# Two changes to a two-layer decoder kernel on one Trainium2 core: two layer norms as a pipeline of quarters, and a quarter of the recurrence's B products moved from GpSimd to ScalarE and TensorE

## The reference

```
def _selective_scan(u, dt, A, Bm, Cm, Dp):      # 4 blocks, 256 channels, 16 states
    dA  = exp(dt[..., None] * A)
    dBu = (dt * u)[..., None] * Bm[:, :, None, :]
    step: h = dA_t * h + dBu_t;  y = einsum('ben,bn->be', h, C_t)
    return y + u * Dp
...
x = x + L1_attn(_layernorm(x))        # four blocks, then a final _layer_norm(x, fn_w, fn_b)
x = x + L1_xattn(ctx_1024, _layernorm(x), mask)
```

## Time and profile before

| | |
|---|---|
| time, median of 3 runs | 1748.06 us (1745.92 to 1748.16) |
| the profiled execution's own time | 1755.21 us |
| its span (first to last instruction) | 1753.4 us |
| recurrence, first scan to last C product | 503.4 to 1348.5 us |
| final norm's stage | from 1356.8 us |
| second cross attention's stage | from 1370.8 us, its first masked score at 1388.9 us |
| busy | DVE 1428.6, PE 1318.3, POOL 1140.6, ACT 1100.6 us |

### The profile page before, as it was taken

How to read it: one execution, slowest core, us unless ns; L and a number is a source line. 1 busy time by engine, 2 the same in 40 slices (tenths; PEclk the granted TensorE clock), 3 DMA queues, 4 the chain that set the end, 5 groups by cost and what they waited for, 6 DMA issues and landing times. The chain is left out here.

```text
span 1753.4 us, 23313 instructions
## 1 busy us (share of the span) xinstructions
PE 1318.3 (75%) x6907; PEld 649.4 (37%) x6907; DVE 1428.6 (81%) x2430; ACT 1100.6 (63%) x2435; POOL 1140.6 (65%) x742
## 2 busy tenths in 40 slices
PE   6787898986666657676576685667655699999989
PEld 4554565553322212222122221222211366666543
DVE  4654888987359999999999999999997588877834
ACT  4444887876566666666666765666743687777730
POOL 2101565651069999999999999999996154444500
PEclk9999999998888888888888888888867899999979
DMA  3000000000054543454543534533430511121000
GB/s 102 1 1 2 1 2 1 1 3 24 6 212 176 193 164 122 169 179 171 194 154 128 195 138 190 194 146 127 176 144 23 175 49 50 50 95 49 1 1 24
DMA packets 70215, 168.03 MB, mean 96 GB/s; under 512 B 20420, under 2 KB 40152, under 8 KB 56664
## 3 DMA queue, kind: packets, MB, share of 16 engines
q1 hardware_dynamic: 68680, 166.17, 25.8%
q10 hardware_dynamic: 1168, 0.53, 0.1%
q0 software_dynamic: 256, 0.01, 0.0%
HBM read 131.04 MB, written 35.65 MB: 95 GB/s over the span
## 5 line engine op out<-in xcount | busy, mean ns | idle before, releaser
L1646 POOL TENSOR_TENSOR ma_hs<-ma_dtuR,ma_Bt 128x1024 f32<-128x1024 f32 x256 | 597.3, 2364 | 7.1 <-DMA ma_dtuR<-ma_dtu_d 6.9
L1829 ACT ACTIVATE ps<-ma_dtR,ma_A 128x512 f32<-128x512 f32 x512 | 332.7, 682 | 297.2 <-DVE ma_hs L1974 254.7
L852 POOL TENSOR_TENSOR x_pr<-x_pr,x_rec 128x512 f32<-128x512 f32 x256 | 267.9, 1047 | 273.5 <-DVE x_rec L1098 273.5
L1968 DVE TENSOR_TENSOR_SCAN ps<-ps,ma_hs 128x1024 f32<-128x1024 f32 x176 | 401.5, 2281 | 0.2
L1723 PE MATMUL ps<-ma_hs,ma_fold 128*32 128x512 f32 x1024 | 176.3, 822 | 206.8 <-POOL ma_hs L1654 178.1
L1064 ACT ACTIVATE x_pr<-x_sm,x_mx 128x256 f32<-128x256 f32 x512 | 255.3, 500 | 69.8 <-DVE x_mx L1089 66.2
L1974 DVE TENSOR_TENSOR ma_hs<-ps,ma_Ct 128x1024 f32<-128x1024 f32 x176 | 215.5, 1224 | 6.1
L1968 DVE TENSOR_TENSOR_SCAN ma_hs<-ps,ma_hs 128x1024 f32<-128x1024 f32 x80 | 182.5, 2281 | 18.4 <-ACT ps L1829 15.5
L1654 POOL TENSOR_TENSOR ma_hs<-ma_hs,ma_Ct 128x1024 f32<-128x1024 f32 x80 | 188.7, 2358 | 11.8 <-DVE ma_hs L1968 11.7
L1690 PE MATMUL ps<-ma_hn,ma_w_tap 128*128 128x512 f32 (+3 forms) x256 | 142.1, 708 | 50.0 <-ACT ma_hn L1853 50.0
L914 PE MATMUL ps<-ident,x_pr 128*128 128x128 f32 x1024 | 161.7, 284 | 5.5 <-DVE x_pT L995 4.4
(11 more groups left out here) (304 smaller groups left out, 2181.1 us busy)
## 6 DMA issues: line engine op xcount, KB each, us to landing
ma_dtuR<-ma_dtu_d SPq DMA_DIRECT2D x32, 1024.0 KB, 6.7
ma_dtR<-ma_dt_d SPq DMA_DIRECT2D x32, 1024.0 KB, 8.9
ma_Bt<-ma_bc_d SPq DMA_DIRECT2D x16, 1024.0 KB, 5.0
ma_Ct<-ma_bc_d SPq DMA_DIRECT2D x16, 1024.0 KB, 7.4
ma_dtu_d<-ma_dtu SPq DMA_DIRECT2D x32, 256.0 KB, 2.0
ma_dt_d<-ma_dt SPq DMA_DIRECT2D x32, 256.0 KB, 2.3
keys_d<-ma_kv SPq DMA_DIRECT2D x32, 256.0 KB, 4.4
values_d<-ma_kv SPq DMA_DIRECT2D x32, 256.0 KB, 3.2
```

Of the source, the lines that this page charges most:

```text
L852: pool.tensor_tensor(pr[:, r, :, :], pr[:, r, :, :], rec[:, r, :].unsqueeze(2).broadcast_to([P, 2, L]), ALU.mult).then_inc(pr_done, 1)
L1646: pool.tensor_tensor(hs[:, k % SLOTS, :, :], dtuR[:, unit(f, h), q, :].unsqueeze(1).broadcast_to([P, 2, CH]), rows(Bt, k), ALU.mult).then_ ...
L1829: e = act.activation(c.ps[:, 2 * (k % 2) + a, :], dtR[:, unit(f, h), q, :], ACT.Exp, scale=A[:, (f // QUARTERS) % 2, h, q, no:no + 1])
L1968: dve.tensor_tensor_scan(out, pair(k), slot(k), 0.0, ALU.mult, ALU.add).then_inc(scan_done, 1)
```

## The change

Two edits. **Norms:** the stage n5 is gone. The cross attention stage runs both norms itself (`TwoNorms`), quarter by quarter over three tiles of its own: the second norm's centre matmul of a quarter starts when VectorE has added that quarter's first norm. GpSimd adds the bias `fn_b` to `xT` beforehand (`shift`), and VectorE does gain and sum in one instruction (`add`). The first projection waits for quarter 0 alone, the first scores for quarter 1; quarters 2 and 3 are scaled on VectorE after the first and second head. The prefetch is issued by the cross attention's SP queue, and the clears (now those of the first cross attention too) move to the norm stage n4 ahead of the recurrence.

**B products:** of a step's 16 B products, the last four (`TURNED` = 12 to 15) are no longer GpSimd's. TensorE turns B and dt x u so that tokens lie on the partitions; ScalarE makes scaled copies of them (`scale_rows`, 32 of 128x128 for a step, spread over t = 0 to 10 by `SCALED`), reading every fourth element and writing every fourth; TensorE turns the products back (`turn_rows`, eight 128x128 transposes for an item) into `pair(k)`. For these items the decays go to `slot(k)`, and the scan takes its inputs from PSUM. The C products are split anew: VectorE's items in a step are 1, 2, 3, 4, 6, 7, 8, 11, 15 (nine), GpSimd's are 0, 5, 9, 10, 12, 13, 14 (seven). `dtR` and `dtuR` hold two halves instead of three.

```diff
+class TwoNorms:
+    def centre(self, pe, n, h):
+        if n:
+            pe.wait_ge(done, self.base + h + 1)
+        pe.matmul(c.ps[:, h, :], c.centre[:, :], (c.xT if n else c.xn)[:, h * CH:(h + 1) * CH], ...)
+    def average(self, pe, n, h):
+        pe.wait_ge(squared, self.base + 4 * n + h + 1)
+        pe.matmul(c.ps[:, 7 - h, :], c.average[:, :], self.sq[:, h, :], ...)
+    def shift(self, pool, h, biased):
+        pool.tensor_tensor(cols, cols, c.fn[:, 1:2].broadcast_to([P, CH]), ALU.add).then_inc(biased, 1)
+    def add(self, dve, h, biased):
+        dve.wait_ge(rstd_done, self.base + h + 1)
+        dve.tensor_tensor(self.shifted[:, h, :], c.ps[:, h, :], self.rstd[:, h, :], ALU.mult).then_inc(scaled, 1)
+        dve.wait_ge(scaled, h + 1)
+        dve.wait_ge(biased, h + 1)
+        dve.scalar_tensor_tensor(out=cols, in0=self.shifted[:, h, :], scalar=c.fn[:, 0:1], in1=cols, ...).then_inc(done, 1)
+    def scale(self, dve, h):
+        dve.wait_ge(rstd_done, self.base + 4 + h + 1)
+        dve.tensor_tensor(c.xn[:, ...], c.ps[:, h, :], self.rstd[:, h, :], ALU.mult).then_inc(done, 1)
 # cross attention, TensorE
+                    for h in range(4):
+                        norms.centre(pe, 0, h)
+                    for h in range(4):
+                        norms.average(pe, 0, h)
+                    norms.centre(pe, 1, 0)
+                    for h in range(3):
+                        norms.centre(pe, 1, h + 1)
+                        norms.average(pe, 1, h)
                     pe.wait_ge(c.wq1_in, 16)
+                    norms.wait(pe, 1)
                 for n in range(NP if small else 1):
                     project(0, n, True, False)
+                if not small:
+                    norms.average(pe, 1, 3)
 # cross attention, ScalarE
+                    square(0,0..3); inv_std(0,0); inv_std(0,1); inv_std(0,2); square(1,0); inv_std(0,3)
+                    square(1,1); inv_std(1,0); square(1,2); inv_std(1,1); square(1,3)
+                    (then the projection's evacuation, inv_std(1,2), inv_std(1,3))
 # recurrence
-    NORM_D = set(range(16)) - {0, 4, 6, 10, 14}
+    NORM_D = set(range(16)) - {0, 5, 9, 10, 12, 13, 14}
+    TURNED = {12, 13, 14, 15}
+    SCALED = (3, 5, 0, 1, 3, 3, 2, 4, 2, 5, 4, 0, 0, 0, 0, 0)
 # GpSimd
-                        if k + AHEAD < NK:
+                        if k + AHEAD < NK and not by_tensor(k + AHEAD):
                             times_b(k + AHEAD)
 # TensorE
+                def turn_rows(k):
+                    pe.wait_ge(rows_done, 32 * (f + 1))
+                    if on_vector(k - 2):
+                        pe.wait_ge(c_vector, n_vector(k - 2) + 1)
+                    else:
+                        pe.wait_ge(scan_done, k - 1)
+                    for a in range(2):
+                        for t in range(4):
+                            mm = pe.transpose(c.ps[:, 2 * (k % 2) + a, t * P:(t + 1) * P],
+                                              rowB[:, t, a, q, :, :].rearrange("p e n -> p (e n)"), c.ident[:, :])
+                    mm.then_inc(turned, 1)
                     if F < NF:
                         pe.wait_ge(dt_done, 2 * F + 2)
+                        turn_b(F)                        # 4 small transposes into PA
 ...
                         kv_job(4 * f + 2, Y[0])
+                    if 0 <= f < NF:
+                        turn_rows(f * ITEMS + 12)
                     if G < NF:
                         if f >= 1:
                             pe.wait_ge(resid, f)
                         average(G)
                     if 0 <= f < NF:
+                        turn_rows(f * ITEMS + 13)
                         sum_y(f, 2)
+                        turn_rows(f * ITEMS + 14)
                         pe.wait_ge(kv_done, 4 * f + 3)
                         kv_job(4 * f + 3, Y[0])
+                    if 0 <= f < NF:
+                        turn_rows(f * ITEMS + 15)
+                    if F < NF:
+                        turn_dtu(F)                      # 4 transposes into PB
 # ScalarE
+                    if by_tensor(k):
+                        act.wait_ge(y_done, (k - SLOTS) // 4 + 1)
+                    elif k >= 2:
 ...
+                def scale_rows(f, i):
+                    t, a, ni = i // 8, i // 4 % 2, i % 4
+                    act.activation(rowB[:, t, a, :, :, ni], dtuT[:, t, :].rearrange("p (e q) -> p q e", q=GQ), ACT.Copy,
+                                   scale=BT[:, f % 2, t, a, ni:ni + 1]).then_inc(rows_done, 1)
+                        if F < NF and t == 9:
+                            copy_b(F)                    # bank PA to BT
+                        if F < NF and t == 15:
+                            copy_dtu(F)                  # bank PB to dtuT
+                        for _ in range(SCALED[t]):
+                            scale_rows(f, made)
```

More of the change, by code:

```diff
@@ L892, in score_pair @@
                         pe.wait_ge(k_in[p], b * 8 + 16 - 8 * p)
+                        if first:
+                            norms.wait(pe, 2)
                     if small and (n >= 4 or not first):
@@ L908, in turn @@
                 def turn(b, n, first):
+                    if not small and first and n < 2:
+                        norms.wait(pe, n + 3)
                     pe.wait_ge(pr_done, b * NH + n + 1)
@@ L1000, in _ @@
             def _(act):
-                norm.on_scalar(act)
+                if small:
+                    norm.on_scalar(act)
+                else:
+                    act.preload_act_table_set("natural_log_exp_and_others")
+                    for h in range(4):
+                        norms.square(act, 0, h)
+                    norms.inv_std(act, 0, 0)
+                    norms.inv_std(act, 0, 1)
+                    norms.inv_std(act, 0, 2)
+                    norms.square(act, 1, 0)
+                    norms.inv_std(act, 0, 3)
+                    norms.square(act, 1, 1)
+                    norms.inv_std(act, 1, 0)
+                    norms.square(act, 1, 2)
+                    norms.inv_std(act, 1, 1)
+                    norms.square(act, 1, 3)
                 def evacuate(b, p, n, first, second):
@@ L1033, in _ @@
                     evacuate(0, 0, n, True, False)
+                if not small:
+                    norms.inv_std(act, 1, 2)
+                    norms.inv_std(act, 1, 3)
                 if small:
@@ L1076, in _ @@
             def _(dve):
-                norm.on_vector(dve)
+                if small:
+                    norm.on_vector(dve)
+                else:
+                    for h in range(4):
+                        norms.add(dve, h, biased)
+                    for h in range(2):
+                        norms.scale(dve, h)
                 def maximum(b, p, n, first):
@@ L1147, in body @@
                         maximum(b, p, n, first)
+                        if masked_rows and first and n < 2:
+                            norms.scale(dve, n + 2)
                         step(b, p, n, first)
@@ L1469, in on_vector, with by_tensor, n_times_b, n_turned @@
         return k % ITEMS in NORM_D
+    def by_tensor(k):
+        return k % ITEMS in TURNED
+    def n_times_b(k):
+        return k - n_turned(k)
+    def n_turned(k):
+        return sum(by_tensor(a) for a in range(k))
     def n_vector(k):
```

176 lines of the change are left out of this document (130 added, 46 removed).

## The result

The changed kernel takes **1736.72 us** (median of 5 runs, 1724.17 to 1738.99) against 1748.06 in the same comparison; the ratio is 0.9914 [0.9886, 0.9943]. The medians lie 11.3 us apart, the ratio stands for 15 us, and its interval (10 to 20 us) holds both. Forecast were 1713 us, a ratio of 0.980, 35 us less: the sign and the range (1693 to 1738) hold, the size doesn't. The profiled execution took 1737.79 us with a span of 1736.1, against 1755.21 and 1753.4 before.

What follows compares the result with a forecast made beforehand. VectorE and GpSimd were both taken as full in the recurrence, with VectorE alone setting the pace after the change. Terms -40 + 10 + 8 + 1 - 13.5 = -35 us gave 1713 us from 1748.1; range 1693 to 1738.

Steps and rivals of the forecast that it cites:

- Norms: Cross attention stage: VectorE starts the first masked score at T+17.2 instead of T+32.1; -13.5 us, from -15 to -9.
- VectorE's gain: Recurrence: VectorE gives up two C products a step, 2.5 us each step, -40 us over 16 steps.
- The B products that remain are in time: GpSimd in the recurrence: products 16 and 17 made 3 us or more before their scans, 18 about 1.3.
- Decay of item 4: ScalarE: late C product 14 delays sum, tap projection, silus and this decay; 0.5 us a step, +8 us, ends 0 and 1.5.
- the gate: VectorE, t = 1: due 5.7 us after scan 0; the awaited sum ends at 4.7, or 6.4 at the lower clock.
- Turn 14: TensorE, behind `sum_y(f,2)`: 0.6 us late for its scan each step, +10 us, ends 0 and 2.5 us a step.
- the first rival: TensorE may stay at 2.4 GHz, so all turns and projections are hidden: 1695 us, chance 0.22.
- the B products' half: Recurrence: -40 + 10 + 8 + 1, forecast at -21 us.
- Scaled copies: ScalarE: 32 copies a step at 0.30 us each, 9.6 us; they cost nothing while VectorE's items cover them.
- ScalarE did not become the bound: Rival on ScalarE: at about 0.55 us a copy it becomes the bound, only norms gain: 1735 us; chance 0.15, shared.
- All hidden: Rival on TensorE: all turns and projections hidden, 1748 - 40 - 13.5 = 1695 us, chance 0.22.
- the sum, 1713: Whole kernel: all terms together give -35 us, 1748.1 - 35 = 1713 us, chance 0.54.

Runs made afterwards that it cites:

- experiment 12: Changed kernel with three filler matmuls before each step's first tap projection and the weights' preparation split and moved behind items 11: 1715.56 us, 0.9806.
- experiment 7: Changed kernel with three extra copies of tap projection 0's first matmul just ahead of it, filling TensorE's idle time before the last sum: 1727.58 us, 0.9874.
- experiment 10: Changed kernel with item 14's C product on VectorE, item 6's on GpSimd, and the weights' preparation split and moved behind items 11: 1708.6 us, 0.9772.
- 8: Changed kernel with item 14's C product on VectorE and item 6's on GpSimd: 1723.8 us, 0.9865.
- experiment 2: Changed kernel with scaled copies contiguous on both sides (products misplaced): 1748.57 us, 0.9994; then only the read contiguous: 1752.25 us, one run.
- experiment 11: Kernel of experiment 10 with scaled copies reading and writing contiguously, B's rows in another order: 1702.35 us, 0.9724.
- 3: Changed kernel with GpSimd's preparation of the next block's weights moved from a step's start to behind item 11 of the same step: 1737.61 us, 0.9946.
- 9: Changed kernel with weights' preparation split: tap weights behind item 11 one step earlier, the rest behind item 11 of the same step: 1733.91 us, 0.9919.
- experiment 4: Changed kernel with the matmul of one key and value job per step issued seven times instead of once: 1747.98 us, 0.9991.

## Why the prediction was right in sign and wrong in size

**Norms** (-13.5; alone 13.5, from 9 to 17): right, and by its own steps, with the first masked score at T+17.2. The full change loses 2 us again at the output projection ahead of T, for which the forecast had nothing.

**VectorE's gain** (-40): right. Items stand 2.20 and 3.46 us apart, and a step without waits is 49.5 us.

**"The B products that remain are in time"**: the step that failed first. The forecast put this term at 0; measured are 12.9 us of waits, 11.0 more than before. I followed GpSimd's queue for products 16 to 18 and not to the two behind them, in front of which the weights' preparation of 5.5 us stands in every fourth step. I had worked out myself that GpSimd's pile at a step's end grows, and used it for the sum alone: the same pile starts the preparation 5.1 to 5.7 instead of 1.3 us after scan 0, so item 3's product comes 2.2 to 3.8 us late and item 4's 1.1, three times. With the other disturbance gone, taking the preparation out of the way gives 12 us (experiment 12 against 7) and 15 us (10 against 8).

**Decay of item 4** (+8, ends 0 to 1.5 us a step): the path is right (late C product 14, late sum, late tap projection 1, late silu), the size is not. In a good step the lateness is 1.71 us against 0.34 in the step shown before, in a long one 2.98. I let the sum slip by 1.5 us and gave 1 of it to slack. With the sum at the higher clock in every step the decay is still 1.76 us late (7), and 0.5 with item 14's product on VectorE (10); so by an estimate from these two the pile costs about 1.25 us a step, and the slack was not there. What I also left out is that TensorE, with no work for 3.1 to 3.7 us ahead of the sum, may run it at the lower clock: 1.7 us for the sum and, at 1250.19, still a little for tap projection 1. Over the run the decays cost 14.5 us more than before instead of 8. At the gate it is 4.3 us more, for which I had allowed none although I had given its end at the lower clock (6.4 against a due time of 5.7).

**Turn 14** (+10): too dear, measured 3.9, of which 2.1 come before scan 13, where I had ruled a wait out. The turns fill TensorE's queue before `sum_y(f,2)`, and in the good steps that sum takes 1.92 us and turn 14 ends with scan 14 on time, as the first rival says. That rival was half right: at this sum the clock stayed up; at the last sum it didn't always.

**The terms together**: B products +11.0, decays +6.5 over the forecast, the gate +4.3, turns -6.1: 15.7 us, against 16 that the B products' half fell short of (21 forecast, 5 measured). That the time still lies in the forecast's range is due in part to the turns, which were over-priced by 6.

**Scaled copies** (0.30 us): measured 0.42, of which 0.13 are the strides by experiment 2; without strides it is 0.29, so the base was right. The Trainium skill's rule in "SBUF — State Buffer", section "Specifications (TRN2)", bears on this: with it I estimated 0.11 us per copy more. The runs agree with that estimate (0.13) for both sides strided, but not for the write alone, which left the distance at 0.29. ScalarE did not become the bound; the price of the strides in time is 6 us, 12 in the recurrence (experiment 11), and only once the disturbances are gone.

**"All hidden", 1695, and the sum, 1713**: experiment 10 comes out at 1708.6 us, with steps of 51.2 where 50.7 were forecast. It shows that the B products' half can give what was forecast for it (the recurrence is 27.7 us shorter than before), but not that the sum was right: item 14's C product is not GpSimd's there, the turns cost 0.8 us instead of 10, and the decays wait at items 4 and 7. That it lies so near 1713 is luck.

What stays open is why, of two steps alike in every row that I compared, one goes on at the higher and one at the lower clock (idle 3.65 and sum 1.92; idle 3.35 and sum 3.64). The rows show the sum at the higher clock in all 14 steps of experiment 7 (idle 0.7 to 1.5 us before it), at the lower or nearly so in the first 14 steps of experiment 2 (idle 4.2 to 4.4, sums 3.19 to 3.64), and both in the change (idle 3.1 to 3.7). The length of the idle time alone does not decide: in the change 1.92 us follow an idle time of 3.65 and 3.64 us follow one of 3.06. Runs of the same kernel may differ by it: the one of 1724.17 us had a mean clock of 0.920, those of 1731.91 to 1738.99 had 0.907 to 0.913; but only one of them has a trace, so that is not shown.

## What to carry to other kernels

Walk each in-order queue through a whole period of the schedule, not one step: work that comes every fourth step was covered only by the lead that GpSimd had at a step's start, and the change took that lead away. Check the releaser that a profile names against the ends of all that the instruction waits for. When one engine's work moves behind another's, look at what TensorE does while it waits: here six of 15 steps were 1.2 to 3.6 us longer where that sum ran slowly (one of them has the preparation in it too), and three filler matmuls a step made the kernel slower by 1.1% where there was next to nothing to fill and faster by 0.4 to 1.1% where there was (experiments 7 and 12). Two mends can hide each other: 3 and 9 gained nothing alone. A cheaper operation on an engine with slack can make the kernel slower (experiment 2); price it again once the real bound is gone (experiment 11).

## What the runs showed of the hardware

A ScalarE copy of 128x128 float32 with a scale operand, issued back to back, takes 0.29 us from start to start with both sides contiguous, 0.29 with one element in 16 bytes written, and 0.42 with both read and written so (experiment 2 and the change, medians of 352 pairs each). The mean duration recorded for one is 0.39, 0.51 and 0.52 us: the stride of the write shows in the duration, and the pace falls only when the read is strided too. The mean busy time of one, 0.32, 0.36 and 0.45, lies between the two and is neither.

The granted clock is worth more by where it is high than by its mean: the profiled run of experiment 4 had 0.93 and took 1747.01 us, that of experiment 10 had 0.922 and took 1708.26.
